# A decoder layer on one core: the first attention in pairs of heads instead of head by head

## The reference, cut to what matters

```python
x = layernorm(x + first_attention(x))              # conv, position, q k v, softmax in bf16, out_w
x = layernorm(x + second_attention(x, context))    # causal self + cross attention, fp32
x = layernorm(x + spline_ffn(x))                   # gates over 8 clusters of 8 tiles, picked spline
# first attention, per batch and head:
p = softmax(q @ k.T / 4)                           # 512 x 512
y = p @ v                                          # 512 x 16
```

## Time and profile before

| | |
|---|---|
| median of 3 runs | 2747.02 us (2743.32 to 2752.6) |
| profiled execution | 2764.27 us, span 2762.5 us |
| PE busy | 2490.1 us (90%), 12674 matmuls |
| DVE busy | 1896.1 us (69%) |
| ACT busy | 1380.5 us (50%) |
| POOL busy | 193.3 us (7%) |
| granted TensorE clock, mean | 0.854 of full speed |
| chain that ended last | PE 80%, DVE 11%, issue 4%, ACT 3%, DMA 1% |

### The profile page before, as it was taken

The page is one execution under the profiler, slowest core; times in us unless marked ns, Lnnn a source line. Parts: engine busy times, 40 slices in busy tenths (PEclk is TensorE's granted clock), DMA queues, the critical chain, the costliest instruction groups (busy, mean ns, idle before and its releaser), DMA issues.

```text
span 2762.5 us, 42501 instructions
## 1 busy us (share of the span) xinstructions
PE 2490.1 (90%) x12674; PEld 1153.5 (42%) x12674; DVE 1896.1 (69%) x5254; ACT 1380.5 (50%) x2945; POOL 193.3 (7%) x353
## 2 busy tenths in 40 slices
PE   5899979999799987999979998899988999889994
PEld 1354324553245433454324543345433454334432
DVE  6668577684777838678386883868748586585844
ACT  2635555355543556345563464724656246563551
POOL 2010000100001000110001100011000110000000
PEclk7699967998689985899859997599975999769996
DMA  4500033000430004200042000510015000240000
GB/s 133 95 9 1 9 61 77 9 2 9 76 63 9 1 10 85 61 1 2 9 92 54 2 1 13 100 42 1 2 29 94 24 1 1 46 84 9 1 1 8
DMA packets 284176, 91.51 MB, mean 33 GB/s; under 512 B 269344, under 2 KB 279712, under 8 KB 283936
## 3 DMA queue, kind: packets, MB, share of 16 engines
q1 hardware_dynamic: 283936, 88.60, 15.9%
HBM read 17.27 MB, written 4.19 MB: 8 GB/s over the span
## 4 chain that ended last, share of the span: by engine, by line
PE 80%; DVE 11%; issue 4%; ACT 3%; DMA 1%; DVEq 0%; POOL 0%; SPq 0%; POOLq 0%; ACTq 0%
PE bank L1256 18%; PE bank L1048 16%; PE bank L1304 12%; PE bank L1290 10%; PE bank L1139 4%; PE bank L1252 4%; PE bank L1149 4%; PE bank L1287 3%; DVE work L659 3%; PE bank L1197 2%; PE bank L1312 2%; PE bank L1269 1%; ACT work L521 1%; PE bank L1087 1%; ACT work L562 1%
## 5 line engine op out<-in xcount | busy, mean ns | idle before, releaser
L562 ACT ACTIVATE work<-bank 128x512 f32<-128x512 f32 (+3 forms) x1536 | 745.6, 553 | 612.6 <-PE bank L1290 270.3
L913 DVE TENSOR_REDUCE top_half<-bank 128x1 f32<-128x512 f32 x1024 | 625.7, 682 | 18.5 <-PE bank L1256 18.5
L1256 PE MATMUL bank<-k_c,q_c 32*128 32x512 f32 x2048 | 626.2, 631 | 0.0
L1290 PE MATMUL bank<-q_c,k_c 32*128 32x512 f32 x2048 | 594.2, 670 | 19.9 <-ACT work L562 19.9
L521 ACT ACTIVATE work<-work,neg 128x512 bf16<-128x512 bf16 x512 | 362.6, 709 | 89.6 <-DVE work L659 54.2
L659 DVE TENSOR_SCALAR_CACHE_REDUCE work<-bank 128x512 bf16<-128x512 f32 x512 | 321.8, 686 | 75.3 <-PE bank L1139 75.3
L1256 PEld LDWEIGHTS bank<-k_c,q_c 32*128 32x128 f32 x2048 | 272.5, 183 | 222.8 <-DVE top_half L913 142.3
L1139 PE MATMUL bank<-k,q 32*128 32x512 bf16 x512 | 249.5, 564 | 110.7 <-DVE work L659 103.2
L1304 PE MATMUL bank<-work,v_flat 128*32 128x512 f32 (+3 forms) x3072 | 336.2, 581 | 6.0 <-ACT work L562 5.8
L1290 PEld LDWEIGHTS bank<-q_c,k_c 32*128 32x128 f32 x2048 | 256.7, 190 | 109.6 <-ACT work L562 74.2
L910 DVE CUSTOM_DVE_ANT_0 masked<-bank,mask_w 128x384 bf16<-128x384 f32 (+3 forms) x512 | 224.1, 488 | 109.0 <-PE bank L1252 102.9
(11 more groups left out here) (176 smaller groups left out, 2436.0 us busy)
## 6 DMA issues: line engine op xcount, KB each, us to landing
xT_pad<-xT SPq DMA_DIRECT2D x16, 256.0 KB, 2.7
ctx_sb<-ctxT SPq DMA_DIRECT2D x8, 512.0 KB, 3.7
x_res<-x SPq DMA_DIRECT2D x8, 512.0 KB, 4.9
out<-y_sb SPq DMA_DIRECT2D x8, 512.0 KB, 2.9
work<-work SPq DMA_TRANSPOSE x128, 4.3
qk_sb<-qkT SPq DMA_DIRECT2D x1, 512.0 KB, 4.7
wq_sb<-Wq SPq DMA_DIRECT2D x1, 512.0 KB, 6.5
wk_sb<-Wk SPq DMA_DIRECT2D x1, 512.0 KB, 7.2
```

The source lines that it names most:

```text
L562: nc.scalar.activation(pT[:, s % PT_SLOTS, g, q0:S], bank[:, RING + n % EXP_RING, 0:S - q0], ACT.Exp, scale=SCALE).then_inc(pT_ready, 1)
L913: nc.vector.tensor_reduce(top_half[:, i % 2, g, u // 2, u % 2:u % 2 + 1], scores, AX.X, ALU.max, negate=True).then_inc(slot_out, 1)
L1256: mm(dst, q_c[rows, i, P * t:P * (t + 1)], k_c[rows, i, S * half:S * (half + 1)], start=True, stop=True, tile_position=(GW * g, 0)).then_i ...
L1290: mm(dst, k_c[rows, i, P * u:P * (u + 1)], q_c[rows, i, :], start=True, stop=True, tile_position=(GW * g, 0)).then_inc(sT_mm, 1)
```

## The change

Heads go in pairs, p = 0 to 7, and within a pair tile by tile, head 2p and head 2p+1 in turn.
- TensorE's scores of a pair alternate between two row groups of the array. The products with the values alternate between two column groups; for that the heads' places in bank 4 are reordered (and out_w's rows on the host, and POOL's copies of v, now 32 of half the size). pv1(p-3) stands behind scores1(p).
- `e1` and `p1T` have four slots instead of three, that is two pairs. `s1` keeps its two halves, one for each head of a pair. One copy and one reciprocal take the sums of a pair.
- ScalarE does exp1(p), then norm1(p-1). The wait for the transposes stands ahead of exp1(p), for both heads of pair p-2.
- The other batch's pieces are put at other places; the spline layer moves behind the last pair and behind the context values; Gelu's product stands apart from the routing scores.
- TensorE's context keys move from before the last products with the values to behind the token product. ScalarE's copies of them follow.
- hT and expertT lie in featB, and the sum with beta is made in place after the spline.

```diff
-    A1_BANKS, E1_SLOTS = 4, 3
+    A1_BANKS, E1_SLOTS = 4, 4
+    HEAD_PAIRS, PAIR = H // 2, 2 * NT
...
 # ScalarE
-                def exp1(h):
-                    if h >= E1_SLOTS:
-                        act.wait_ge(p1T_in[h % E1_SLOTS], transposed(b, h - E1_SLOTS))
+                def exp1(p):
+
+                    for e in range(2):
+                        h = 2 * p + e
+                        if h >= E1_SLOTS:
+                            act.wait_ge(p1T_in[h % E1_SLOTS], transposed(b, h - E1_SLOTS))
                     for t in range(NT):
...
-                for h in range(H):
-                    exp1(h)
-                    if h >= 1:
-                        norm1(h - 1)
-                    if h == 12:
+                for p in range(HEAD_PAIRS):
+                    exp1(p)
+                    if p >= 1:
+                        norm1(p - 1)
+                    if p == 6:
                         out1(0)
...
-                norm1(H - 1)
+                norm1(HEAD_PAIRS - 1)
+                if prev:
+                    compress(c)
+                out1(1)
                 context_keys()
-                out1(1)
...
 # VectorE
                 scores1(b, 0)
                 scores1(b, 1)
-                if prev:
-                    second_residual(c, sf)
-                for h in range(H):
-                    sum1(h)
-                    norm1(h)
-                    if h + 2 < H:
-                        scores1(b, h + 2)
+                for p in range(HEAD_PAIRS):
+                    sums1(p)
+                    norm1(p)
                     if prev:
-                        if h == 0:
+                        if p == 0:
+                            second_residual(c, sf)
+                        if p == 3:
+                            cluster_choice(c, sf)
+                        if p == 4:
+                            expert_choice(c, sf)
+                    if p + 2 < HEAD_PAIRS:
+                        scores1(b, p + 2)
...
                 for i in range(CTX_PAIRS):
                     values(i)
                 if prev:
+                    spline(c, sf)
                     third_sums(c, sf)
...
 # TensorE
-                for h in range(2, H):
-                    scores1(h)
-                    if h >= 5:
-                        pv1(h - 5)
+                for p in range(2, HEAD_PAIRS):
+                    scores1(p)
...
+                    if p >= 3:
+                        pv1(p - 3)
...
-                pv1(H - 5)
-                pv1(H - 4)
+                pv1(HEAD_PAIRS - 3)
                 for i in range(CTX_PAIRS):
                     values(i)
-                pv1(H - 3)
-                if prev:
-                    pe.wait_ge(spline_done, b * NT)
-                context_keys()
-                pv1(H - 2)
-                pv1(H - 1)
+                pv1(HEAD_PAIRS - 2)
+                pv1(HEAD_PAIRS - 1)
                 pe.wait_ge(vj_evac, b * PAIRS + CTX_PAIRS)
                 if ahead:
                     position(b + 1)
                 pe.wait_ge(tok_ready, (b + 1) * KD)
                 token_out(out_sb, 0, out_mm)
+                if prev:
+                    pe.wait_ge(spline_done, b * NT)
+                context_keys()
                 pe.wait_ge(ck_evac, (b + 1) * CTX_UNITS)
```

More of the change, by code:

```diff
@@ L435, in first_values @@
                     for a in range(4):
[L436 to L439, removed]
+                        for half in range(2):
+                            src = v_nat[RH * q:RH * (q + 1), half::2, :].rearrange("p g (t a j) -> p g t a j", t=4, a=4)[:, :, :, a, :]
+                            dst = v1[RH * a:RH * (a + 1), :, :, :].rearrange("p (g q) t j -> p g q t j", q=4)[:, half::2, q, :, HD * half:HD * (half + 1)]
+                            nc.gpsimd.tensor_copy(dst, src).then_inc(v1_ready, 1)
+                pool.wait_ge(v1_ready, (b + 1) * 32)
                 own_wait(nc.gpsimd)
@@ L878, in batch @@
                 if prev:
-                    last_sums(c, sf)
+                    third_norm(c)
+                if ahead:
+                    add_position(b + 1)
                 dve.wait_ge(xn_in, b * 16 + 16)
@@ L893, in batch @@
                 ln_apply(0, b, normalized(0, x_res, x_res))
+                if prev:
+                    last_norm(c)
+                    sf.end()
                 if ahead:
@@ L1142, in pv1 @@
-                def pv1(h):
-                    pe.wait_ge(p1T_in[h % E1_SLOTS], transposed(b, h))
-                    if h == 8:
+                        for e in range(2):
+                            h, n = 2 * p + e, PAIR * p + 2 * t + e
+                            i, rows = h // GH, slice(GW * (h % GH), GW * (h % GH + 1))
+                            if n >= A1_BANKS:
+                                pe.wait_ge(s1_evac, b * H * NT + n - A1_BANKS + 1)
+                            mm(bank[:, n % A1_BANKS, :], q_1[rows, i, P * t:P * (t + 1)], k_1[rows, i, :], start=True, stop=True,
+                               tile_position=(GW * (h % GH), 0)).then_inc(s1_mm, 1)
@@ L1146, in pv1 @@
+                def pv1(p):
+                    for e in range(2):
+                        pe.wait_ge(p1T_in[(2 * p + e) % E1_SLOTS], transposed(b, 2 * p + e))
+                    if p == HEAD_PAIRS // 2:
                         pe.wait_ge(o1_copied, b * KD + 1)
-                    g = h // 2 % 4
                     for j in range(4):
-                        last = mm(bank[GW * g:GW * (g + 1), 4, :], v1[:, h, j, :], p1T[:, h % E1_SLOTS, :, j, :],
-                                  start=(h % 2 == 0 and j == 0), stop=(h % 2 == 1 and j == 3), tile_position=(0, GW * g))
@@ L1151, in pv1 @@
-                    last.then_inc(o1_mm, 1)
+                        for e in range(2):
+                            h = 2 * p + e
+                            g, half = h % GH, h // GH % 2
+                            last = mm(bank[GW * g:GW * (g + 1), 4, :], v1[:, h, j, :], p1T[:, h % E1_SLOTS, :, j, :],
+                                      start=(half == 0 and j == 0), stop=(half == 1 and j == 3), tile_position=(0, GW * g))
+                            if j == 3:
+                                last.then_inc(o1_mm, 1)
```

139 lines of the change are left out of this document (65 added, 74 removed).

## The result

| | before | after |
|---|---|---|
| median of 4 runs | 2747.93 us | 2884.22 us (2879.93 to 2891.51) |
| span of the profiled execution | 2762.5 us | 2889.8 us |
| PE busy | 2490.1 us | 2404.7 us |
| granted TensorE clock, mean | 0.854 | 0.836 |

The changed kernel is slower: 1.0499 times the time before, 95% interval 1.0467 to 1.0530. That is +136 us by the medians and +127 us by the two profiled executions, against the +109 us of the prediction. (The profiled execution of before lies 16 us above its median, that of the changed kernel 7 us above its own.) TensorE's busy time fell by 85 us, and nothing of that arrived at the end.

The account below looks back on a forecast made before the run. The prediction took tightly coupled TensorE and VectorE to bound the first attention before, and ScalarE's wait for transposes after. 34 + 6 x 11.6 + 5.7 = +109 us on the 2747.0 median gave 2856 us, range 2820 to 2905.

Parts of the forecast that it names:

- Part 2: First attention: ScalarE's exps wait for both transposes of the pair just normalized, a loop of 13.2 us per pair.
- stage, batches 1 to 6: ScalarE's exps in the first attention: the last exp ends at 1128.5 instead of 1124.3 in batch 3, +4.2 us.
- context keys: TensorE, between token product and next q, k and v: the moved keys cost their full length, +7.1 us per batch.
- batch 0 / each of 1 to 6, first exp to first exp: Whole batches: +34 us for batch 0, which has no other work mixed in, and +11.6 us for each of 1 to 6.
- batch 7: Last batch: +4.5 us at the stage's end, keys hidden behind LayerNorm but for 1.2, together +5.7 us.
- packing on TensorE: Scores and products with the values of two heads side by side: no gain credited, 0 us.
- Part 3: End of stage: the last four transposes queue at 2.2 us spacing, the token product starts 4.5 us later.
- the addition of 1.0 us for the load next to pair 1: First attention: the x_res load, issued next to pair 1, slows a transpose beside it, +1.0 us.
- The 1.3 us for the table load: ScalarE, first attention: the Exp table load behind Gelu stands after the wait for the transposes, +1.3 us.
- the unknown on the clock: End of stage: TensorE's clock after pauses, bounds 0 to +23 us per batch; taken as 0 beyond the old dip.
- VectorE's pace: Rival, first attention: transposes do not gate ScalarE, VectorE's busy time sets the stage; -64 us, 2683 us, chance 0.04.
- The clock stays low: Rival, end of stage: TensorE at half clock for 10 to 20 us, +7 per batch, 2905 us, chance 0.18.

Follow-up runs that it names:

- experiment 3: Changed kernel with ScalarE's two loop calls exchanged, norm1(p-1) ahead of exp1(p): 2781.43 us, ratio 1.0107 to the kernel before.
- experiment 5: Changed kernel with norm1(p-1) ahead of exp1(p) and both heads of a pair in one row and column group, so no packing: 2767.23 us, ratio 1.0023.
- experiment 6: experiment 3 plus the other batch's last pieces earlier and the context keys back ahead of the last products with the values: 2707.11 us, ratio 0.9808.
- experiment 9: experiment 6 with ScalarE's order of the change put back, exp1(p) ahead of norm1(p-1): 2826.96 us, ratio 1.0262.
- experiment 7: experiment 6 with the context keys again behind the token product, and ScalarE's copies behind out1(1): 2812.21 us, ratio 1.0189.
- experiment 4: Changed kernel with both heads of a pair in the same row and column group, so their matmuls can't run side by side: 2876.97 us, ratio 1.0455.
- experiment 2: Kernel before with only the context keys moved behind the token product, and ScalarE's copies behind out1(1): 2788.75 us, ratio 1.0134.
- experiment 8: experiment 6 with both heads of a pair in one row group and one column group: 2722.98 us, ratio 0.9880.

## Why the prediction was right, and where its sizes were off

**The direction and the cause hold.** Part 2, ScalarE waiting for the transposes of the pair just normalized, is shown from both sides: the gate alone, put on the old kernel, cost 303 us (305 expected), and its removal from the changed kernel gave back 103 us. The loop was 13.4 us (predicted 13.2). Batch 0's stage grew by 27.1 us, exactly as worked out (139.9 - 48.4 = 91.5); that it is exact is luck, since the 1.0 us added there for the load did not come, and the loops were each 0.2 us longer.

Term by term, predicted and measured:

| term | predicted | measured |
|---|---|---|
| loop per pair | 13.2 | 13.4 |
| stage, batches 1 to 6 | +4.2 | +5.1 |
| last landing after last exp | 11.9 | 12.9 |
| token product, distance from the last exp (17.2 before) | 17.5 | 18.7 to 19.9 |
| context keys | +7.1 | +7.0 and 0.9 of wait |
| token product itself, batches 1 to 6 | 0 | -1.2 |
| batch 0 / each of 1 to 6, first exp to first exp | +34 / +11.6 | +37.6 / +14.3 |
| batch 7 | +5.7 | +4.9 |
| packing on TensorE | 0 | nothing that can be told |

**The terms that were mis-sized.** First, the last four transposes in Part 3. I took 2.2 us between issues; in batch 3 the issues stand at 0.9, 2.5, 6.1 and 8.3 us behind the last exp, and the last landing at 12.9. In batches 1 to 6 the three distances add up to 7.3 to 7.5 us, where I had 6.6. Both engines had normalized all four heads by 2.5 us behind the last exp. What spaces the issues is SyncE itself: its four instructions last 1.32 to 3.27 us, and each starts some 0.3 us behind the end of the one before. The view of these four (duration in ns, least/median/most; first and last start):
```profile
L340 SPq DMA_TRANSPOSE work<-work x4: 1318/2084/3268, 1196.2 to 1203.7; - x4
```
Why one lasts 3.27 us and another 1.32 is not shown by any run.

Second, the addition of 1.0 us for the load next to pair 1. It did not come: the exps around it start 13.4 us apart like the others. The 1.3 us for the table load did (14.7 us at pair 7).

Third, the unknown on the clock, which I set to 0 beyond the old dip. Position took 4.3 to 5.5 us in batches 1 to 6 instead of 3.7, and the last pair's products 1.89 where they take 1.04 at the full clock. But the old dip itself went away: the token product took 3.62 us in all six, where before it took 5.41 in four of them. In batch 3 the two nearly cancel, +2.3 and -1.8.

Together, per batch 1 to 6: stage +5.1, start of the token product behind the last exp +1.8, the token product itself -1.2, keys with their wait +7.9, rest +0.7, which makes +14.3. The forecast had 4.2 + 0.3 + 0 + 7.1 + 0 = 11.6. Batch 7 came near by luck: its stage grew by 4.4 and its end by 7.8, and its rest was 7.3 shorter. So the traces are 18 us over the forecast; the other 9 of the 27 by the medians come from how far each profiled execution lies above its median.

The Trainium skill ("TensorE: Matmul & The Clock Gate", section Part 1) says that an idle TensorE falls to the half clock and regains the full one with sustained work; this end agrees, since the lower level begins at the end of the 4.53 us pause (1202.9) and the full one comes back in work without a gap (0.99 from 1213 on).

**The rivals.** "VectorE's pace" was to hold if the transposes didn't gate ScalarE. They do; with the gate taken out (experiment 3) ScalarE waits for VectorE, as that rival says, but the stage is 3.4 us shorter than before, not 15, and that with the last pieces moved out of it. "The clock stays low" was right in place, not in size: in batch 3 the products and position took 2.3 us more, not 7, and the token product gave 1.8 of it back. Packing: the Trainium skill ("TensorEngine Tiling (Array Packing)", section PSUM Bottleneck) says that packing speeds TensorE and not the emptying of PSUM, by which VectorE would be next. In the kernel as changed the DMA came before VectorE. In experiment 3 TensorE waits 187.7 us for VectorE, which agrees; but experiment 5 is no slower without packing, so this case doesn't show that packing is what put VectorE next.

**Where the kernel stands.** The change held two things: a pairwise order, for which no gain in the stage is shown (65.0 against 64.4 us in batch 0, where no other work is mixed in, and 88.5 against 88.7 in the others with all pieces inside, experiment 6), and two placements, of which that of ScalarE's norm costs 110 us of stage and end, and that of the keys 77 us of end (experiments 9 and 7, each against experiment 6). With both placed elsewhere, and the other batch's pieces earlier, the pairs are 1.9% faster than the kernel before. Of the 56 us between the two traces, 39 lie in the ends and 17 in the rest. Whether single heads with the pieces placed so would do as well was not tried, so nothing here shows that the pairs are needed for it.

**Left open.** The rest of the batches, which none of the experiments' edits touches, varied between 1763 and 1803 us over the traces, in steps of some 3 to 5 us a batch. The clock records of the traces show what goes with it. I summed the time that the rest spent at the lower level: 131 us in experiment 4 (rest 1763.0), 155 in experiment 6 (1771.5), 197 in the kernel before (1788.6), 240 in experiment 7 (1802.9). All twelve traces lie near one line, with some 0.37 us of time for each us at the lower level. So the rest differs by the clock; what decides on the clock was not tested. The lower level comes mostly in the last 40 us of the second attention, where TensorE is busy:
```profile
1307.00:1317.00 10.00, 9.33 (x64) 3.48 (x61) 1.80 (x4) 6.24 (x14) 0.00 (x0) 1.00 0.01 2
1317.00:1327.00 10.00, 9.31 (x40) 3.89 (x44) 0.00 (x0) 5.55 (x11) 0.00 (x0) 0.66 0.01 2
```
This is experiment 6, batch 3: TensorE is busy 9.3 of 10 us in both, and the clock falls in the second, at 1319.5. The gaps ahead of the fall are 0.67 us each, and no pause like that of 4.53 us stands there. Of the 40 us ahead of the next batch's first exp the lower level takes 10 here, and 19 in experiment 7; half of that difference is nearly the 5 us a batch by which the rest of experiment 7 is longer. For this reason the sums of stage and end are the better measure of an edit here than the whole, and 20 us of the whole can come or go with the rest.

## What to carry to other kernels

When two engines and a DMA pass a buffer around, write down which instruction on the engine stands between the cause of a transfer and the wait for it. With a pair as the unit, the same distance takes six slots instead of four (not tried), or the other order (experiment 3): issue what starts the transfer before the work that has to wait for the transfer before it. And a block of TensorE's work that stands in a wait costs its own length when it is moved out, and can cost more: it lengthens the path (+7.3 us a batch in experiment 2), and the hole that it leaves can lower the clock of what follows (+10.4 in experiment 7). Last, when work moves out of a stage, a shorter stage says nothing until the work is counted where it went.

## What the runs showed of the hardware

- The two DMA transposes of a pair (128 x 2048 bf16 each), right behind each other, started 1.6 to 3.1 us apart in the changed kernel, where SyncE's own instruction for one lasts 1.3 to 3.4 us. They landed 4.3 to 5.3 us after their issue, apart from three that took 5.5 to 6.4. In the first pair of batch 3 (issued 1114.18 and 1116.17) the second landed 4.9 us after its issue, so the pair was back 6.9 us after its first issue.
- Two matmuls in two column groups took half the time at either clock: eight products in 1.89 us at the lower level and 1.04 us at the full one, where experiment 4, without packing, took 3.54 and 1.89 us. Its timeline of TensorE, batch 3 (the first group at a granted clock of 1.00, the second at 0.5):
```profile
1192.73 1.89 PE L1165 MATMUL bank<-work,v 128*32 128x512 bf16 x8 [2.10 <-DMA work<-work]
1197.97 3.54 PE L1165 MATMUL bank<-work,v 128*32 128x512 bf16 x8 [3.35 <-DMA work<-work]
1201.44 3.70 PE L1059 MATMUL bank<-xs,pe_sb 128*128 128x512 f32 x8
```
- Less work for TensorE did not raise the clock but came with a lower one. Mean granted clock of the profiled executions, with packing and without: 0.836 and 0.861 (the change and experiment 4), 0.857 and 0.875 (experiments 3 and 5), 0.870 and 0.877 (experiments 6 and 8); the other runs of these kernels differ in the same way. I had not expected that the change, with its shorter products, could have a lower clock than before (0.854). Of the two timelines ahead of the token product, the one without packing had position at the full clock (3.70 us), the one with packing partly at the lower one (5.10). What links the two was not tested.
